# A fused GNN kernel on one core: the twelve-turn loops of ScalarE and VectorE begin two turns later

## The reference, cut to what matters

```python
# x: 3125 nodes x 128; 53125 edges (src, dst) with 128 features each
agg  = segment_sum(mlp([x[src], x[dst], edge]), dst)     # 384 -> 256 -> 256 -> 128
agg += segment_sum(mlp([x[dst], x[src], edge]), src)
s1 = gru(x, agg); s2 = gru(agg, s1); s3 = gru(s1, s2)
x = layernorm(x + s3)
for l in range(3):                                       # X starts as x
    S = segment_sum(X[src], dst); Z = (1 + eps[l]) * X + S
    X = relu(Z @ W1[l] + b1[l]) @ W2[l] + b2[l]
out = layernorm(x + X)
```

## Time and profile before

| | |
|---|---|
| median of 3 runs | 2449.35 us (2448.73 to 2454.7) |
| profiled execution | 2454.33 us, span 2452.2 us |
| busy share of the span: PE, DVE, POOL, ACT | 94%, 69%, 54%, 50% |
| mean granted clock of TensorE | 0.977 of full speed |
| ACT's wait before h (L590) with no releaser ("issue") | 40.8 us in 6 waits |
| PE's wait for ACT's sd (L554) | 25.3 us in 6 waits |

### The profile page before, as it was taken

The page is one execution under the profiler, slowest core; times in us unless marked ns, Lnnn a source line. Parts: engine busy times, 40 slices in busy tenths (PEclk is TensorE's granted clock), DMA queues, the critical chain, the costliest instruction groups (busy, mean ns, idle before and its releaser), DMA issues. The chain is left out here.

```text
span 2452.2 us, 42170 instructions
## 1 busy us (share of the span) xinstructions
PE 2299.6 (94%) x12735; PEld 1915.7 (78%) x12735; DVE 1702.2 (69%) x3628; ACT 1220.9 (50%) x2106; POOL 1333.8 (54%) x846
## 2 busy tenths in 40 slices
PE   5999999999999999999999999999999859699996
PEld 3887887888788878878887887888888735488785
DVE  7877877878778878877877887887878546602114
ACT  4555555556556655655655555555656414211112
POOL 3676777667667766766776677667767400000000
PEclk8999999999999999999999999999999979899998
DMA  4456555445555445555455555355555460295863
GB/s 154 84 112 119 96 100 95 88 84 110 93 93 101 93 79 99 104 94 94 89 90 93 106 96 96 74 103 99 106 93 102 61 220 1 105 365 232 347 274 146
DMA packets 233802, 293.68 MB, mean 120 GB/s; under 512 B 125755, under 2 KB 191294, under 8 KB 225228
## 3 DMA queue, kind: packets, MB, share of 16 engines
q1 hardware_dynamic: 160457, 237.91, 35.0%
q0 software_dynamic: 73216, 54.58, 17.4%
HBM read 219.35 MB, written 73.05 MB: 119 GB/s over the span
## 5 line engine op out<-in xcount | busy, mean ns | idle before, releaser
L445 POOL DMA_INDIRECT sums<-outb,target x416 | 675.2, 1623 | 477.4 <-ACT outb L608 225.3
L438 POOL DMA_INDIRECT xg<-in_x,gidx x416 | 653.9, 1572 | 160.7 <-issue 140.6
L590 ACT ACTIVATE h<-ebank,b2c 128x512 f32<-128x512 f32 x416 | 287.6, 691 | 377.7 <-PE ebank L1151 336.9
L1162 PEld LDWEIGHTS ebank<-w3t,h 128*128 128x128 f32 x3328 | 404.1, 192 | 13.8
L1162 PE MATMUL ebank<-w3t,h 128*128 128x128 f32 x3328 | 404.9, 275 | 0.0
L1151 PE MATMUL ebank<-h1h,w2h 128*128 128x512 f32 x832 | 368.8, 443 | 3.9 <-DVE h1l L805 3.9
L1151 PE MATMUL ebank<-h1h,w2l 128*128 128x512 f32 x832 | 332.0, 399 | 0.0
L1151 PE MATMUL ebank<-h1l,w2h 128*128 128x512 f32 x832 | 331.7, 399 | 0.0
L584 ACT ACTIVATE h1h<-hpre 128x512 fp32r<-128x512 f32 x416 | 237.9, 623 | 88.2 <-DVE hpre L800 87.7
L805 DVE SCALAR_TENSOR_TENSOR h1l<-hpre,h1h 128x512 fp32r<-128x512 f32 x416 | 258.6, 680 | 0.0
L1137 PE MATMUL ebank<-sdh,w1h 128*128 128x512 f32 x624 | 247.6, 397 | 2.1 <-DVE sdl L826 1.5
(11 more groups left out here) (254 smaller groups left out, 4005.6 us busy)
## 6 DMA issues: line engine op xcount, KB each, us to landing
ring<-adj SPq DMA_DIRECT2D x54, 1568.0 KB, 8.0
rowb<-along SPq DMA_DIRECT2D x104, 512.0 KB
adj<-band SPq DMA_DIRECT2D x25, 1500.0 KB, 14.5
ef<-in_edge_attr SPq DMA_DIRECT2D x103, 256.0 KB, 2.7
stay<-adj SPq DMA_DIRECT2D x6, 1568.0 KB, 14.4
xg<-in_x,gidx POOLq DMA_INDIRECT x416
sums<-outb,target POOLq DMA_INDIRECT x416
xw<-in_x SPq DMA_DIRECT2D x104, 40.0 KB
```

The lines of the kernel that those rows point to most:

```text
L438: pool.indirect_dma_start(out=to, out_offset=None, in_=a["x"], in_offset=bass.IndirectOffsetOnAxis(ap=ids, axis=0)).then_inc(s_x[par], 16)
L445: pool.indirect_dma_start(out=tables[k % 2], out_offset=bass.IndirectOffsetOnAxis(ap=target[par][:, 1, k:k + 1], axis=0), in_=outb[par][:, ...
L590: nc.scalar.activation(h2[:, way, f, :], bank[6 + f][:, :], ACT.Relu, bias=b2c[:, f:f + 1]).then_inc(s_h2, 1)
L1162: last = nc.tensor.matmul(bank[6 + way][:, t * P:(t + 1) * P], h2[:, way, k, t * P:(t + 1) * P], w3t[:, k, :], start=False, stop=(t == K - ...
```

## The change

A constant AHEAD = 10 sets how many turns ACT and DVE write out ahead of their loops; it was 8 in effect. The loops then run over turns 10 to 93, and the last ten turns are written out. Each turn keeps its operations, its order and the turns in which it clears, waits (`fresh`) or wraps; only the form in which the numbers are written differs. The six jumps back of both engines come between the turns 21 and 22, 33 and 34, 45 and 46, 57 and 58, 69 and 70, 81 and 82. PE, POOL and SP are as they were.

```diff
--- before.py
+++ after.py
@@ -59,6 +59,7 @@
 BACK = 16
 SPAN = 80
 NB_A = 16
+AHEAD = 10
 assert G == 4 * ITERS and WIDE <= 512
 ADUMMY = NR * AW
 ASIZE = -(-(ADUMMY + P) // P) * P
@@ -649,13 +650,13 @@
                     upper_e(0)
                 first(0)
                 if win:
-                    for g in range(8):
-                        turn(g, g % 2, g // 2, early=g < 2, cleared=(1, -1, g % 4 - 1) if g > 4 else None)
+                    for g in range(AHEAD):
+                        turn(g, g % 2, g // 2, early=g < 2, cleared=(g // 4, g // 4 - 2, g % 4 - 1) if g > 4 and g % 4 else None)
                     with act.Fori(0, ROUNDS) as m:
-                        for q in range(12):
-                            turn(m * 12 + (8 + q), q % 2, m * 6 + (4 + q // 2),
-                                 cleared=(m * 3 + (2 + q // 4), q // 4, q % 4 - 1) if q % 4 else None)
-                    for g in range(8 + 12 * ROUNDS, G):
+                        for g in range(AHEAD, AHEAD + 12):
+                            turn(m * 12 + g, g % 2, m * 6 + g // 2,
+                                 cleared=(m * 3 + g // 4, g // 4 - 2, g % 4 - 1) if g % 4 else None)
+                    for g in range(AHEAD + 12 * ROUNDS, G):
                         turn(g, g % 2, g // 2, ahead=min(2, G - 1 - g),
                              cleared=(g // 4, g // 4 - 2, g % 4 - 1) if g % 4 and g // 4 < ITERS - 1 else None)
                 else:
@@ -976,13 +977,13 @@
                 window(1, 1)
                 ways(0)
                 places(0, 0, early=True)
-                for g in range(8):
-                    turn(g, g % 2, g // 2, early=max(0, 2 - g))
+                for g in range(AHEAD):
+                    turn(g, g % 2, g // 2, early=max(0, 2 - g), fresh=(g // 4 - 1) * 3 if g == 8 else None)
                 with dve.Fori(0, ROUNDS) as m:
-                    for q in range(12):
-                        turn(m * 12 + (8 + q), q % 2, m * 6 + (4 + q // 2),
-                             fresh=m * 9 + (q // 4 + 1) * 3 if q % 4 == 0 else None, wrapped=m if q == 3 else None)
-                for g in range(8 + 12 * ROUNDS, G):
+                    for g in range(AHEAD, AHEAD + 12):
+                        turn(m * 12 + g, g % 2, m * 6 + g // 2, fresh=m * 9 + (g // 4 - 1) * 3 if g % 4 == 0 else None,
+                             wrapped=m if g == 11 else None)
+                for g in range(AHEAD + 12 * ROUNDS, G):
                     turn(g, g % 2, g // 2, ahead=min(2, G - 1 - g), fresh=(g // 4 - 1) * 3 if g % 4 == 0 else None,
                          wrapped=ROUNDS if g == 11 + 12 * ROUNDS else None)
```

## The result

The changed kernel takes 2415.42 us in the median of 4 runs (2412.7 to 2416.59); the kernel before, run beside it, 2451.56 us (4 runs). The ratio is 0.985 (95% interval 0.9838 to 0.9862), 1.5% faster. I had said 2417 us, in a range of 2410 to 2432. The profiled execution took 2414.69 us.

What follows compares the result with a forecast made beforehand. The prediction took PE, busy 94% of the span, to bound the kernel. Removing the old jumps gave -35.0 us and the new ones +3.0 us; 32.0 us off the median made 2417 us, range 2410 to 2432 us.

Steps and rivals of the forecast that it cites:

- What the six jumps cost, 35.0 us: Jump turns 20, 32, ..., 80: they take 35.0 us more than six ordinary 17.9 us turns, all saved by the change.
- The flush holds up the fetch: At ACT's old jumps: the instruction fetch comes through only when the flush has drained, making jumps 6 to 8 us.
- The jump at its new place, 3.0 us taken: Head of turns 22, 34, ..., 82: each jump takes 3.0 us, from POOL's 2.6 us plus 0.4 us by choice.
- The new jumps' price for PE, +3.0 us: Turns 22, 34, ..., 82: PE loses 0.5 us at each of six new jumps, +3.0 us in all.
- The clock: PE's clock at the new jumps: stays at 1.00, nothing added; if it fell, up to 10 us again.
- A fixed price for the jump: Rival: ACT's and DVE's jumps cost 6 to 8 us wherever they stand; time within a few us of 2449; chance 0.07.
- a fetch that takes turns with the flush packet by packet: Rival rule: DMA engines go round queue rows packet by packet, so the flush causes no wait; time stays 2449 us.
- The partial effect, two engines in each other's way: Rival at the new jumps: two engines fetching at once make a jump 5 us; time 2438 us; chance 0.09.
- The waits for POOL's adds: Rival behind the six flushes: without PE's pause DVE waits 4.3 us each for POOL's adds; 2443 us; chance 0.02.
- The fetch behind POOL's indirect DMAs: Rival around turn 22: the fetch waits for POOL's gathers and adds, jumps 9 us; time 2462 us; chance 0.03.

Runs made afterwards that it cites:

- (5): Kernel before the change, loops left in place, SP's flush issued behind the loads of one group later: 2421.99 us, ratio 0.987 to the kernel before.
- (1): Changed kernel with both loops beginning at turn 12, so jumps come right behind a turn that issues a flush: 2442.83 us, ratio 0.9968 to the kernel before.
- (6): Kernel before the change with each flush cut in two, 96 of 128 partitions at the old time, 32 a turn later: 2428.05 us, ratio 0.9897.
- (3): Changed kernel with DVE's loop back at turn 8, ACT's at 10, so only DVE jumps behind the flush: 2445.68 us, ratio 0.9973 to the kernel before.
- (4): Changed kernel with ACT's loop back at turn 8, DVE's at 10, so only ACT jumps behind the flush: 2451.33 us, ratio 0.9995 to the kernel before.
- (7): Changed kernel with all 104 turns of ACT and DVE written out, no loop and no jump: 2415.39 us, ratio 0.9847 to the kernel before.

## Why the prediction was right

- **What the six jumps cost, 35.0 us.** Right. The same 72 turns are 35.1 us shorter, and the jumps that were added instead cost next to nothing.
- **The number.** 2417 us is nearer to 2415.42 than the working deserves. I had forecast 32.0 us less than a median of 2449.35; measured are 36.1 us less than 2451.56. A saving that was 4 us too small met a starting point that was 2 us too low.
- **The flush holds up the fetch.** Right, and now shown: moving the flush alone (5) frees the jump, moving the jump behind another flush (1) stops it again, and a smaller flush (6) stops it for less. To the letter, "only when the flush has drained" was too strong: in the kernel before, the first instruction packet starts 1.8 to 3.1 us before the landing, while the last part of the flush still moves. ACT goes on 2.0 to 3.1 us behind that start, so the end of the wait and the landing fall close together. The landing to 0.1 us was good luck in the two rows shown; over the six jumps of the kernel before ACT goes on between 0.3 us ahead of it and 0.4 us behind it, and in experiment 1 up to 1.9 us ahead.
- **The jump at its new place, 3.0 us taken.** Too long. ACT's takes 2.5 us at the first and sixth, and POOL's took 2.6 us. The 0.4 us added for two engines that fetch at once was wrong for ACT: with DVE's jump beside it ACT's takes 2.5 us, and without it (3) as much. DVE's own takes 2.8 to 2.9 us, and so it does alone (4), 2.8 to 3.1 us.
- **The new jumps' price for PE, +3.0 us.** This term was mis-sized with the length before it. At 2.5 us the slack that I had read off turn 22 (1.8 us at the bank, 0.81 and 0.26 us before `sdl`, 0.36 us at PE) holds it nearly whole: the six new jump turns take 0.3 us more than six of 17.9 us, and the version with no jumps (7) is no faster. With 0 us in place of 3.0 the saving is 35.0 us, against 36.1 us measured between the medians.
- **The clock.** Right that it would not fall: the granted clock is 1.00 at the jump and in the 6 us behind it, where 0.50 followed PE's pause.
- **The rivals.** A fixed price for the jump is excluded by 5 and 6, and 6 speaks against a fetch that takes turns with the flush packet by packet, as do the 1158 packets of SP's queue that start in a stretch of 5 us with no instruction packet among them. The partial effect, two engines in each other's way, is excluded by 3 and 4, in which a single engine waits as long as both. The waits for POOL's adds did not come in the flush turns: turn 20 takes 17.8 us. The fetch behind POOL's indirect DMAs did not show either, at a DMA share of 0.19.

Why the DMA engines let the flush go first stays open. The trace doesn't say which engine an instruction packet ran on, so whether it waits for that one engine's share of the flush is not shown. No run here tells whether it is the number of the flush's packets, their size, their target in HBM, or all 16 engines being taken at once, and no other large transfer was put beside a jump.

## What to carry to other kernels

A jump back in a long loop (430 and 849 instructions here) can need a small DMA, here one packet of 8 KB per engine and 2.5 to 2.9 us in a quiet time, and that DMA waited behind a flush of 1500 KB that happened to be in flight. SP's jump, 0.4 us with no packet of q14 beside it, shows that not every jump does. Look for waits with the releaser "issue" that come once per loop iteration, compare them with the landing of the nearest bulk DMA, and put either the jump or the transfer a turn away; all engines that jump there must move, not one. A late start costs nothing where the turn has that much slack (1.5 us here), so count the slack before writing the loop out.

## What was not expected of the hardware

The jump of an engine alone is no shorter than that of two at once: 2.5 us for ACT in both cases, and behind a flush 7.8 us for ACT alone and 8.7 us for DVE alone, against 7.9 us for ACT and 8.1 us for DVE together. And instructions fetched in sequence cost nothing, though a flush is in flight a fifth of the time (15 us of every four turns, 71.6 us) and none of their packets starts in its first 9 us (7): in these kernels only the jump is exposed.
